# Attention beside the projections of the sequence after next: one copy of a group's maxima, the second query, the keys, the smear, the positions and the extra rows at later places, and a preparation with fewer, wider loads

## What is computed

```python
h = gru(norm(x)*gamma+beta, w_ih, w_hh, b_ih, b_hh); y = h @ w_out.T + b_out       # 512 steps, 256 states
y = experts with LoRA, the first of 8 by argmax(x @ gate_W.T + gate_b)
q, k, v, p, y = split(norm(x) @ W_in.T + b_in)                                     # 16 heads of 16
k = (1 - smear) * k + smear * k_prev
pos = cumsum(sigmoid(y)); mask = causal - (pos_i - pos_j)
attn = softmax(q/s @ (k/s).T / 4 + mask); out = norm(silu(p) * (attn @ v) @ W_out.T)
y = (silu(x @ w_gate.T) * (x @ w_up.T)) @ w_down.T
```

## Time and profile before

| | |
|---|---|
| median of 3 runs | 1505.95 us (1502.7 to 1507.28) |
| the profiled execution | 1511.65 us, span 1509.4 us |
| busy: PE, DVE, ACT, POOL | 1299.7, 1151.1, 855.4, 403.3 us |
| preparation | until about 23 us |
| attention | about 960 to 1430 us |

### The profile page before, as it was taken

One profiled execution on the slowest core, in us unless ns is written; L12 is line 12 of the kernel. 1 busy time (PEld: TensorE's weight loads), 2 busy tenths in 40 slices (PEclk: granted clock), 3 DMA queues, 4 the chain that ended last, 5 costly groups with the idle time before them and its releaser, 6 DMA issues. The chain is left out here.

```text
span 1509.4 us, 64193 instructions
## 1 busy us (share of the span) xinstructions
PE 1299.7 (86%) x26361; PEld 971.4 (64%) x26361; DVE 1151.1 (76%) x5180; ACT 855.4 (57%) x2991; POOL 403.3 (27%) x754
## 2 busy tenths in 40 slices
PE   5888888888888888888888885589999999999986
PEld 4677777777777777777777774245555555555543
DVE  5778888888888888888888885867677677677475
ACT  3555555444555445554555552347777777777864
POOL 2101111111111111111111112552553553522454
PEclk9999999999999999999999996779999999999998
DMA  5200000000000000000000000394662672660001
GB/s 121 40 4 6 6 7 5 6 7 5 6 7 6 5 7 6 7 5 6 7 6 5 7 5 8 100 145 88 111 108 49 108 108 51 106 88 1 2 21 35
DMA packets 68937, 53.60 MB, mean 36 GB/s; under 512 B 12686, under 2 KB 68390, under 8 KB 68646
## 3 DMA queue, kind: packets, MB, share of 16 engines
q1 hardware_dynamic: 66470, 49.32, 19.0%
q10 hardware_dynamic: 2176, 0.20, 0.1%
HBM read 31.84 MB, written 15.47 MB: 31 GB/s over the span
## 5 line engine op out<-in xcount | busy, mean ns | idle before, releaser
L759 PE MATMUL PS<-GQ,W 128*128 128x32 f16 x12288 | 497.0, 177 | 103.1 <-DVE GQ L1127 87.4
L759 PEld LDWEIGHTS PS<-GQ,W 128*128 128x128 f16 x12288 | 415.8, 96 | 207.2 <-DVE GQ L1127 199.7
L1012 ACT ACTIVATE RQ<-PS 128x16 f32<-128x16 f32 x512 | 102.6, 200 | 342.3 <-PE PS L759 342.1
L2564 DVE TENSOR_REDUCE MX<-PS 128x1 f32<-128x512 f32 (+3 forms) x352 | 218.8, 634 | 87.1 <-PE PS L2005 85.1
L2290 ACT ACTIVATE PT<-PS 128x512 f32<-128x512 f32 (+1 forms) x352 | 193.3, 566 | 104.3 <-PE PS L2021 101.1
L1118 DVE TENSOR_TENSOR_SCAN PS<-RQ,PS 128x64 f32<-128x64 f32 x512 | 151.3, 295 | 81.8 <-ACT RQ L1012 68.8
L828 PE MATMUL PS<-W 128*128 128x256 f16 x1024 | 196.2, 273 | 0.0
L1001 ACT ACTIVATE GB<-GQ 128x32 f16<-128x32 f16 x512 | 171.8, 336 | 0.4 <-DVE GQ L1132 0.4
L718 POOL TENSOR_TENSOR rt<-mv,eps 128x1 f32<-128x1 f32 x93 | 17.8, 192 | 500.9 <-DVE mv L1141 500.9
L1014 ACT ACTIVATE ZB<-PS 128x16 f32<-128x16 f32 x512 | 95.2, 186 | 90.2 <-PE PS L759 90.1
L2002 PE MATMUL PS<-KS,QS 99*128 99x256 bf16 (+3 forms) x512 | 133.7, 313 | 11.0 <-DVE MX L2564 9.2
(11 more groups left out here) (487 smaller groups left out, 2836.5 us busy)
## 6 DMA issues: line engine op xcount, KB each, us to landing
QS<-q_parts SPq DMA_DIRECT2D x90, 128.0 KB, 9.6
KS<-k_parts SPq DMA_DIRECT2D x90, 128.0 KB, 12.4
q_parts<-PQ SPq DMA_DIRECT2D x16, 384.0 KB, 10.2
k_parts<-PK SPq DMA_DIRECT2D x16, 384.0 KB, 3.2
X<-XM SPq DMA_DIRECT2D x32, 64.0 KB
out_dram<-X SPq DMA_DIRECT2D x8, 256.0 KB, 2.3
XM<-in_L_attn_x_dram SPq DMA_DIRECT2D x16, 80.0 KB
s_hh<-in_L_attn_w_hh_dram SPq DMA_DIRECT2D x1, 768.0 KB, 5.8
```

The lines of the kernel that those rows point to most:

```text
L759: return pe.matmul(bank[:, p, at:at + WIDE].rearrange("p (r b) -> p r b", b=B), W[:, kc, w:w + P], state[:, kc, :, part].unsqueeze(1).to_b ...
L2564: dve.tensor_reduce(MX[:, g % 2, heads[0]:heads[-1] + 1, NT - 1 - it], p_x[:, k % 2, 0:len(heads) * w].rearrange("p (a w) -> p a w", w=w), ...
```

## The change

The first four units of x come as four transfers of one unit each, issued by ACT (units 0 and 1 ahead of beta and the bias columns, units 2 and 3 behind them, under a semaphore that DVE waits for at its end); gamma moves to the semaphore of the late loads. DVE does the statistics before the maxima of w_ih and gamma, and YN before the scales. wb is made by POOL, behind the row scales and in front of the attention's constants. W1 and W2 are made in two halves. In attention the fourth row of maxima is copied at k = 0 of the group that uses it, and the steps of `project_qk` move: second query on ACT from 9 to 10 and in POOL's `split` from 10 to 11, PE's key products from 9 and 10 to 10 and 11, ACT's keys from 10 and 11 to 12 and 13, smears from 11 and 12 to 13 and 14, positions from 12, 13, 14 to 14, 15, 16, DVE's extra rows from 17, 18, 19 to 18, 19, 20, their turn from 21 to 22 and the copy KAT from 22 to 23.

```diff
@@ preparation, loads
+        def load_unit(eng, j, done):
+            eng.dma_start(XM[:, j, :], x_by_step[:, :, j, :]).then_inc(done.sem, 16)
 
...
-                for t in range(0, GS, 2):
-                    load_x(sp, t, 0, X_FIRST, loads_x0)
...
-            N_LATE = 14
+            N_LATE = 15
@@ preparation, GpSimd, behind the scales of rows 0 and 1
+                pool.wait_ge(loads_gb.sem, 48)
+                pool.wait_ge(loads_ih.sem, 16)
+                pool.tensor_tensor(wb[:, :, :], s_ih[:, :, :], bet[:, :].unsqueeze(1).to_broadcast([P, 6, D]), ALU.mult).then_inc(bias_v.sem, 1)
@@ preparation, ScalarE
-                col(gam[:, :], gamma_d, 1)
+                act.dma_start(gam[:, :], gamma_d.rearrange("(c p) -> p c", c=1),
+                              allow_slow_non_contiguous=True).then_inc(loads_late.sem, 16)
+                for j in range(2):
+                    load_unit(act, j, loads_x0)
...
-                for t in range(1, GS, 2):
-                    load_x(act, t, 0, X_FIRST, loads_x0)
+                for j in range(2, X_FIRST):
+                    load_unit(act, j, loads_x2)
...
-                act.activation(flat(W1), flat(whhT), ACT.Copy, scale=S_gru).then_inc(high_w.sem, 1)
+                for kc in range(HC):
+                    act.activation(W1[:, kc, :], whhT[:, kc, :], ACT.Copy, scale=S_gru).then_inc(high_w.sem, 1)
@@ preparation, VectorE
-                dve.wait_ge(loads_ih.sem, 16)
-                dve.tensor_reduce(mx[:, 1:2], flat(s_ih), AX.X, ALU.max, apply_absolute_value=True).then_inc(reduced.sem, 1)
-                dve.wait_ge(loads_gb.sem, 64)
-                dve.tensor_reduce(mx[:, 2:3], gam[:, 0:1], AX.X, ALU.max, apply_absolute_value=True).then_inc(reduced.sem, 1)
-                dve.wait_ge(turned.sem, 3)
-                dve.tensor_scalar(whhT[:, :, 2 * H:], PS[:, 2, :].rearrange("p (k n) -> p k n", k=HC), 0.5, None,
-                                  ALU.mult).then_inc(kept_n.sem, 1)
-                dve.wait_ge(loads_x0.sem, 16 * GS)
...
+                dve.wait_ge(loads_ih.sem, 16)
+                dve.tensor_reduce(mx[:, 1:2], flat(s_ih), AX.X, ALU.max, apply_absolute_value=True).then_inc(reduced.sem, 1)
+                dve.wait_ge(loads_late.sem, 16)
+                dve.tensor_reduce(mx[:, 2:3], gam[:, 0:1], AX.X, ALU.max, apply_absolute_value=True).then_inc(reduced.sem, 1)
+                dve.wait_ge(turned.sem, 3)
+                dve.tensor_scalar(whhT[:, :, 2 * H:], PS[:, 2, :].rearrange("p (k n) -> p k n", k=HC), 0.5, None,
+                                  ALU.mult).then_inc(kept_n.sem, 1)
...
-                dve.tensor_tensor(wb[:, :, :], s_ih[:, :, :], bet[:, :].unsqueeze(1).to_broadcast([P, 6, D]), ALU.mult).then_inc(bias_v.sem, 1)
...
-                dve.wait_ge(high_w.sem, 1)
-                dve.scalar_tensor_tensor(flat(W2), flat(whhT), S_gru, flat(W1), ALU.mult, ALU.subtract).then_inc(low_w.sem, 1)
-                dve.wait_ge(high_w.sem, 2)
+                for kc in range(HC):
+                    dve.wait_ge(high_w.sem, kc + 1)
+                    dve.scalar_tensor_tensor(W2[:, kc, :], whhT[:, kc, :], S_gru, W1[:, kc, :], ALU.mult, ALU.subtract).then_inc(low_w.sem, 1)
+                dve.wait_ge(high_w.sem, HC + 1)
...
+                dve.wait_ge(loads_x2.sem, 32)
@@ attention, body
                                     rows_of_maxima(*group(g + 1), k, group(g - 1))
+                                if k == 0:
+                                    rows_of_maxima(b, p, g, None, None)
@@ attention, GpSimd project_qk
-                    for c in {8: (0,), 10: (1,), 14: (2,), 16: (3,)}.get(i, ()):
+                    for c in {8: (0,), 11: (1,), 14: (2,), 16: (3,)}.get(i, ()):
@@ attention, TensorE project_qk
-                    for c in {6: (0,), 8: (1,), 9: (2,), 10: (3,)}.get(i, ()):
+                    for c in {6: (0,), 8: (1,), 10: (2,), 11: (3,)}.get(i, ()):
...
-                    for n in {12: (0, 1), 13: (2,), 14: (3,)}.get(i, ()):
+                    for n in {14: (0, 1), 15: (2,), 16: (3,)}.get(i, ()):
...
-                    if i == 21:
+                    if i == 22:
@@ attention, ScalarE project_qk and rows_of_maxima
-                    for c in {7: (0,), 9: (1,), 10: (2,), 11: (3,)}.get(i, ()):
+                    for c in {7: (0,), 10: (1,), 12: (2,), 13: (3,)}.get(i, ()):
...
-                    if i == 22:
+                    if i == 23:
...
-                    for i in {8: (0,), 9: (1,), 10: (2, 3)}.get(k, ()):
+                    for i in {8: (0,), 9: (1,), 10: (2,), None: (3,)}.get(k, ()):
@@ attention, VectorE project_qk
-                    for c in {11: (0,), 12: (1,)}.get(i, ()):
+                    for c in {13: (0,), 14: (1,)}.get(i, ()):
...
-                    if i == 17:
+                    if i == 18:
...
-                    if i == 18:
+                    if i == 19:
...
-                    if i == 19:
+                    if i == 20:
```

More of the change, by code:

```diff
@@ L233, in build @@
         loads_late = signal("loads_late")
+        loads_x2 = signal("loads_units_2_3")
         X_FIRST, X_NEXT = 4, 12
@@ L404, in _ @@
                     act.activation(whhT[:, i, 0:2 * H], PS[:, i, :], ACT.Copy).then_inc(kept.sem, 1)
-                act.wait_ge(loads_gb.sem, 64)
+                act.wait_ge(loads_late.sem, 16)
                 for i, (first, last) in enumerate(((0, 4), (4, 6))):
@@ L427, in _ @@
                 dve.tensor_reduce(mx[:, 0:1], flat(s_hh), AX.X, ALU.max, apply_absolute_value=True).then_inc(reduced.sem, 1)
-                dve.wait_ge(loads_ih.sem, 16)
-                dve.tensor_reduce(mx[:, 1:2], flat(s_ih), AX.X, ALU.max, apply_absolute_value=True).then_inc(reduced.sem, 1)
-                dve.wait_ge(loads_gb.sem, 64)
-                dve.tensor_reduce(mx[:, 2:3], gam[:, 0:1], AX.X, ALU.max, apply_absolute_value=True).then_inc(reduced.sem, 1)
-                dve.wait_ge(turned.sem, 3)
-                dve.tensor_scalar(whhT[:, :, 2 * H:], PS[:, 2, :].rearrange("p (k n) -> p k n", k=HC), 0.5, None,
-                                  ALU.mult).then_inc(kept_n.sem, 1)
-                dve.wait_ge(loads_x0.sem, 16 * GS)
+                dve.wait_ge(loads_x0.sem, 32)
                 for j in range(2):
@@ L452, in _ @@
                                   ALU.bitwise_and).then_inc(sc_v.sem, 1)
-                dve.tensor_tensor(wb[:, :, :], s_ih[:, :, :], bet[:, :].unsqueeze(1).to_broadcast([P, 6, D]), ALU.mult).then_inc(bias_v.sem, 1)
-                dve.wait_ge(sc_p.sem, 2)
-                dve.tensor_scalar(kscale[:, 0:1], PS[:, 6, 0:1], 2.0 ** -15, None, ALU.mult).then_inc(sc_v.sem, 1)
-                dve.tensor_scalar(kscale[:, 1:2], PS[:, 6, 0:1], 2.0 ** -14, None, ALU.mult).then_inc(sc_v.sem, 1)
-                dve.tensor_scalar(kscale[:, 3:4], PS[:, 6, 0:1], -2.0 ** -14, None, ALU.mult).then_inc(sc_v.sem, 1)
-                dve.wait_ge(sc_v.sem, 8)
-                dve.reciprocal(kscale[:, 2:3], kscale[:, 1:2]).then_inc(sc_v.sem, 1)
                 dve.wait_ge(rstd.sem, 3)
@@ L464, in _ @@
                                       ALU.subtract, ALU.mult).then_inc(y_ready.sem, 1)
+                dve.wait_ge(sc_p.sem, 2)
+                dve.tensor_scalar(kscale[:, 1:2], PS[:, 6, 0:1], 2.0 ** -14, None, ALU.mult).then_inc(sc_v.sem, 1)
+                dve.tensor_scalar(kscale[:, 0:1], PS[:, 6, 0:1], 2.0 ** -15, None, ALU.mult).then_inc(sc_v.sem, 1)
+                dve.wait_ge(sc_v.sem, 6)
+                dve.reciprocal(kscale[:, 2:3], kscale[:, 1:2]).then_inc(sc_v.sem, 1)
+                dve.tensor_scalar(kscale[:, 3:4], PS[:, 6, 0:1], -2.0 ** -14, None, ALU.mult).then_inc(sc_v.sem, 1)
                 dve.wait_ge(bias_v.sem, 1)
@@ L470, in _ @@
                 dve.tensor_tensor(bih[:, 0:4], bih[:, 0:4], bhh[:, 0:4], ALU.add).then_inc(bias_v.sem, 1)
+                dve.wait_ge(sc_v.sem, 8)
                 dve.tensor_scalar(BC[:, 4:6], bhh[:, 4:6], S_gru, 0.5, ALU.mult, ALU.mult).then_inc(bias_v.sem, 1)
@@ L536, in build @@
             hv = Signal(reduced.sem, 1, 4)
-            hv_ps = Signal(high_w.sem, 1, 2)
+            hv_ps = Signal(high_w.sem, 1, 3)
             wsc = Signal(sc_v.sem, 1, 9)
             wsc_ps = Signal(sc_p.sem, 1, 2)
-            wsplit = Signal(low_w.sem, 1, 2)
+            wsplit = Signal(low_w.sem, 1, 3)
             r_ps = signal("r_ps")
@@ L591, in build @@
             laT_ps = signal("loraT_ps")
-            rows96 = Signal(loads_x0.sem, 1, 16 * GS)
+            rows96 = Signal(loads_x0.sem, 1, 32)
             laT = signal("loraT_ready")
@@ L595, in build @@
             inter = signal("inter_high_ready")
-            ilow = Signal(loads_gb.sem, 3, 64)
+            ilow = Signal(loads_gb.sem, 3, 48)
             xl = Signal(loads_ih.sem, 1, 16)
@@ L1592, in build @@
             x4 = signal("x4_ready")
-            stored = signal("stored", 16)
+            stored = Signal(loads_x2.sem, 16, 32)
             def turn(b, c):
@@ L1721, in _ @@
```

(2 more changed lines are left out.)

1 line of the change is left out of this document (removed).

## The result

The changed kernel takes **1513.2 us** (median of 4 runs, 1511.67 to 1513.71) against **1504.64 us** for the one before (4 runs, 1502.7 to 1507.28; the 1505.95 above is the median of three of them): ratio 1.0048, 95% interval 1.0028 to 1.0068, slower by some 8.6 us. The profiled execution took 1513.71 us with a span of 1511.6. Before's profiled execution, 1511.65, lies 7 us above its own median, so the two traces differ by 2.1 us only. The first question is therefore what of before's trace belongs to that execution and not to the kernel.

The account below looks back on a forecast made before the run. The prediction took PE in attention, busy 294.1 of 317.0 us in its middle, as the bound. Its terms, -3.0 - 0.5 + 5.1 + 4.8 + 2.6 = +9.0, gave 1515 us on the median, range 1500 to 1525.

Parts of the forecast that it names:

- +5.1: Attention, query, keys, smear and positions: 0.85 us longer in each of six sequences, in us in all.
- +4.8: Attention, extra rows: PE waits 0.95 us longer for KAT in each of five sequences, in us in all.
- Bound, and that the waits stay: Attention: what moves PE there moves the end, and PE's wait for the smeared keys is not gone after the moves.
- first rival: Attention: the keys' wait and its two slow stretches vanish and KAT finds slack, giving 1492 us; chance 0.16.
- Start, -3.0: Preparation before the recurrence: x landing earlier ends the block 3.0 us early, between 2.0 and 3.9.
- The rule of exclusion: Preparation: two-port or two-SBUF-input Vector instructions and GpSimd instructions exclude each other; start gives 3.0 us with it, 3.9 without.
- What would show it: Expected signs: waits for KK over 1.1 us, KAT 1.2 us, recurrence starting at about 20.4, YN ending behind wb.
- Fourth row, -0.5: Attention, group turns: the copy changes places with an exponential, PE's wait moves one place, gaining 0.5 us in all.
- Query, keys, smear, positions, +0.85 a body: Attention: wait before the position matmuls 0.35 us longer, then waits for maxima at places 17 to 19.
- GpSimd, "so nothing": Attention, place 21: the gating product starts 1.2 us later, PE is 0.85 later with 0.35 to spare, no cost.
- Extra rows, +0.95 a body: Attention, place 24: KAT stands behind one more exponential and OT's copy, so PE waits 0.95 us longer.
- Clock, +2.6: Attention: longer stalls bring two more stretches of PE at 1.2 GHz, 1.3 us each, 2.6 us in all.

Follow-up runs that it names:

- e7: Changed preparation with before's attention, only PE's position sums moved from places 12 to 14 to 14 to 16: 1503.21 us, ratio 0.9996.
- e1: The changed kernel with all attention tables set back to before's, so the new start alone: 1501.44 us, ratio 0.9988.
- e5: The changed kernel with the second query copied at place 9 and split at place 10 again: 1510.06 us, ratio 1.004.
- e11: e1 with keys, smears and positions moved, but not the second query, fourth row or extra rows: 1503.21 us, ratio 0.9996.
- e3: The kernel before with only the extra rows, their turn and the copy KAT one place later: 1510.29 us, ratio 1.005.
- e4: The kernel before with only second query, keys, smears and positions moved as in the change: 1514.5 us, ratio 1.0064.
- e6: The kernel before with only the fourth row of maxima copied at the next group's first place: 1506.36 us, ratio 1.0012.
- e8: e1 with the two bias columns on another semaphore, so that wb waits for beta alone: 1503.61 us in one execution.
- e12: e8 with wb made by VectorE behind the scales and no product on GpSimd: 1502.04 us, ratio 0.9979.
- e2: The preparation of before with all the moves of the attention: 1517.0 us, ratio 1.0088.
- e9: e8 with the first column of each key made by VectorE in front of the smear, not by ScalarE: 1501.23 us, ratio 0.9984.
- e10: e9 with PE's turn at place 21 waiting for two of KA's four steps: 1502.09 us, ratio 0.999.

## Why the prediction came out as it did

The forecast was 1515, +9.0; measured +8.6. The two terms that carry the sum, +5.1 and +4.8, were right in where TensorE would wait. That the sum is so close is luck: it is too high by a clock term of 2.6 and by waits for maxima of 0.5 in six bodies, which didn't come, and too low by 0.8 to 1.3 at the start and by a wait at place 21 that was put at nothing and costs some 0.9 in five bodies.

- **Bound, and that the waits stay.** Right: places of attention set the time, and moving the steps behind PE's wait moved the wait along. e7 shows why the first rival (1492) fails: the wait for the key can be removed whole, and nothing is won.
- **Start, -3.0.** Mis-sized: -1.73 in the profiled execution, -2.2 in the mean of five traces. The rule of exclusion held, but three landings were later than the step had them: s_hh 0.6 (7.21), x's statistics 0.9 (9.32 for 8.4), and the bias column, which set wb at 12.65 and not 11.4. Also, not YN but a 1x1 step of the scale's chain stood under wb (in e1, e5, e7 and e11 it was YN). "What would show it" was wrong in this detail and in the 20.4: the first multiplication came at 21.64.
- **Fourth row, -0.5.** Wrong in sign when it stands alone: +0.38 a body with the wait for KA at place 21, +0.08 without it. The step looked at the turn of the group and not at place 22, where KAT stands behind the same row. Inside the whole change it is part of an interaction: e3, e4 and e6 sum to +3.2 a body, together they make +1.96. Of the difference, 0.6 is the second query at place 12, and 0.66 is the row: alone it costs 0.38, in the change it costs nothing at place 25 and gives 0.28 back at places 35 and 38. The +2.25 at place 25 is 0.41 from the keys, the wait of 0.82 at place 21 and the 0.98 of the extra rows, 2.21 in all.
- **Query, keys, smear, positions, +0.85 a body.** Mis-sized: +0.41. The first position matmul of the third sequence stands 19.94 us into its body, 1.96 later than before; the forecast had 1125.4 - 1105.51 = 19.9. With 1.57 of work moved ahead of it, 0.39 is lost, where the forecast had 0.35. (The wait for the key itself isn't longer, 1.04 beside 1.10, as PE arrives later by its wait of 0.2 for the second query too.) The other 0.5, waits for maxima at places 17 to 19, didn't come: the table stays at +0.41 from place 17 to 21, and PE has no wait of 0.15 us or more between the positions and place 21. The step from +0.05 to +0.41 between places 15 and 17 is work, the other sums of positions, which stood two places earlier.
- **GpSimd, "so nothing".** Wrong: +0.50 at place 21 against e1's body, which waits 0.35 there already; in all a wait of 0.82 us for KA's last step, which runs beside the product and ends 0.24 behind it. The product came 1.46 later against a forecast 1.2, and PE only 0.41 later against 0.85: what had been over-counted for PE was the cover that hid the product. The two errors cancel by luck, 0.91 for 0.85 a body.
- **Extra rows, +0.95 a body.** Right in mechanism, mis-sized: +1.34 between places 24 and 25. ACT is "without a gap" there because KAT fills the time until PE has place 23's scores, and PE is late with them by its wait for KA. The two slots are the forecast's 0.95; the 0.4 is what a wait at place 21 costs once KAT stands behind that exponential (e3).
- **Clock, +2.6.** Wrong: the changed attention ran at 2.4 GHz from 999 us on (PEclk 1.00) with stalls as long and more of them. With the tables of before, the attention had three low stretches in one execution (before, bodies 2, 4 and 7), one in another (e1, body 7) and none in e8 and e12; with the changed tables none in one (changed) and one in another (e2, body 3). They belong to executions, at least in the main, and the forecast's term had nothing to stand on. Whether the order of the steps makes them rarer isn't shown: the one in body 7 is in before, e1, e6, e9 and e10 and in no trace in which the keys, the extra rows or the positions were moved.

## What to carry to other kernels

A step that is moved pays at the next shared bank or queue behind it, so follow each queue it stands in (here the second query through GpSimd to the gating product, the row through ScalarE to KAT) to the next place where TensorE waits. Removing the largest wait of a table can gain nothing, if the other engines are as long in the same stretch: look at what they do during the wait before pricing it. And subtract place by place between unchanged parts of two traces before any total; one execution can hold several microseconds that are no part of the kernel. Take more than one body to subtract from: a wait that costs nothing in one order (here 0.35 us for KA) costs its full length once something later in the chain hangs on it.

## What the runs showed of the hardware

- **A one-element instruction on VectorE can be held for a whole product on GpSimd.** A step of mrow with two SBUF operands, 1x1, takes 0.15 us alone and took 1.65 (changed), 1.46 (e8), 1.46 (e9) and 1.15 (e10) beside wb, each time ending within 0.02 us of wb's end; the 1x1 `tensor_scalar` beside wb took 0.14 (e1, e7). The Trainium skill ("SBUF — State Buffer", Who interferes with whom) has this rule for two SBUF inputs; the traces agree, and show that one element is enough. In attention the last step of KA, 128x64, takes 2.37 us beside the 2.35 of the gating product and 0.58 behind it. A cast with one SBUF input can be held too: KA's third step took 2.47 us in e1, where it began 0.04 behind the product, and 0.26 in e8, where it began 0.03 behind it. The record of YN in e1 ends 0.8 us behind wb; why isn't settled.
- **A gap in front of a loop.** The interval from step 16 to step 17 of the recurrence was 1.72 us without a gap (e1, e5), 2.95 in the changed kernel, 4.51 in before and 5.15 in e8, put down to "issue". In these five its size goes with how long the transfers of x still ran: DMA share from 48 to 52 and from 52 to 56 us 0.00 and 0.02 in e5, 0.32 and 0.01 in e1, 0.50 and 0.02 changed, 0.63 and 0.61 before, 0.63 and 0.26 in e8. But e2 had 0.64 and 0.29 with an interval of only 2.13. That instructions are fetched late behind those transfers is argued, not shown; the Trainium skill ("Runtime: NRT & Kernel Launch", Instruction fetch mechanics) says that a taken branch to a target outside the two pages held forces a fetch of the target page by DMA before execution goes on. This gap (up to 3.4 us) and the low stretches (1.3 us each in bodies of before, 0.7 in e2, 2.2 in body 7) are large enough for the few microseconds between runs of one kernel; that they make them isn't shown, since one execution of each was profiled.
